# Score products of the first sixteen attention groups on all 128 rows, with each head's keys alone in a cleared buffer

## The reference

```python
x = x + layernorm(attention(layernorm(x), wq, bq, wk, bk, wv, bv, wo, bo))
x = x + layernorm(experts(layernorm(x), Ws, bs, Wg, Wu, Wd))
```

## Time and profile before

| | us |
|---|---|
| median of 3 runs | 924.04 (924.03 to 924.41) |
| the profiled execution | 925.53 |
| its span, first to last instruction | 923.4 |
| TensorE busy (share of the span) | 769.0 (83%) |
| VectorE busy | 629.2 (68%) |
| ScalarE busy | 556.9 (60%) |
| GpSimd busy | 471.1 (51%) |
| mean granted TensorE clock | 0.79 |
| mean rate of the DMA engines | 72 GB/s |

### The profile page before, as it was taken

One profiled execution on the slowest core, in us unless ns is written; L12 is line 12 of the kernel. 1 busy time (PEld: TensorE's weight loads), 2 busy tenths in 40 slices (PEclk: granted clock), 3 DMA queues, 4 the chain that ended last, 5 costly groups with the idle time before them and its releaser, 6 DMA issues. The chain is left out here.

```text
span 923.4 us, 21865 instructions
## 1 busy us (share of the span) xinstructions
PE 769.0 (83%) x6606; PEld 447.4 (48%) x6607; DVE 629.2 (68%) x2328; ACT 556.9 (60%) x1101; POOL 471.1 (51%) x540
## 2 busy tenths in 40 slices
PE   3568886789999999988998899898977999999930
PEld 1122232333333335554554455466865878778720
DVE  3855668778877787888889787755644555555546
ACT  3589887675666567665676577555543444444427
POOL 3575647475352445675366447757544223333227
PEclk9555555555555569998999899899997999999975
DMA  5343323315601011122111212212333532323248
GB/s 173 126 121 98 120 77 112 91 38 187 223 24 30 25 41 16 22 48 53 19 30 31 41 19 43 53 25 45 56 73 84 110 41 40 46 34 47 34 104 283
DMA packets 69243, 66.52 MB, mean 72 GB/s; under 512 B 5536, under 2 KB 62752, under 8 KB 69152
## 3 DMA queue, kind: packets, MB, share of 16 engines
q1 hardware_dynamic: 55872, 50.86, 17.9%
q0 software_dynamic: 13280, 14.49, 11.2%
HBM read 34.04 MB, written 31.29 MB: 71 GB/s over the span
## 5 line engine op out<-in xcount | busy, mean ns | idle before, releaser
L1035 DVE CUSTOM_DVE_ANT_0 unused<-bank,mask 128x384 f16<-128x384 f32 (+3 forms) x512 | 235.9, 485 | 83.8 <-PE bank L1408 80.7
L894 ACT ACTIVATE pT<-bank 128x512 f16<-128x512 f32 (+1 forms) x384 | 201.7, 533 | 108.9 <-PE bank L1417 105.8
L1417 PE MATMUL bank<-qT,kT 32*128 32x384 f16 (+3 forms) x512 | 176.3, 390 | 29.3 <-ACT pT L894 27.4
L1408 PE MATMUL bank<-kT,qT 32*128 32x384 f16 (+3 forms) x512 | 178.6, 398 | 8.2 <-DVE nmax L1035 7.7
L681 POOL TENSOR_SCALAR_AFFINE_SELECT pT<-pT 128x512 f16<-128x512 f16 x128 | 84.7, 706 | 129.1 <-ACT pT L894 128.4
L1837 POOL DMA_INDIRECT expert_rows<-y_sb,dest x36 | 56.0, 1555 | 118.8 <-DVE y_sb L1956 113.3
L1510 PE MATMUL bank<-tile_xT,gu_part 128*128 128x256 f16 (+1 forms) x616 | 90.0, 287 | 11.7 <-DVE stage L1219 11.6
L2031 PE MATMUL bank<-xT,gu_part 128*128 128x256 f16 (+1 forms) x792 | 94.7, 277 | 2.4 <-issue 1.4
L1417 PEld LDWEIGHTS bank<-qT,kT 32*128 32x128 f16 x512 | 39.5, 97 | 117.3 <-issue 60.6
L1448 PEld LDWEIGHTS bank<-va,pT 128*128 128x128 f16 x1280 | 49.4, 102 | 91.6 <-issue 66.7
L2031 PEld LDWEIGHTS bank<-xT,gu_part 128*128 (+1 forms) x792 | 77.9, 101 | 18.0 <-issue 3.7
(11 more groups left out here) (198 smaller groups left out, 1439.7 us busy)
## 6 DMA issues: line engine op xcount, KB each, us to landing
expert_rows<-tile_in SPq DMA_DIRECT2D x1, 8192.0 KB, 26.5
stage<-wg SPq DMA_DIRECT2D x8, 688.0 KB, 4.1
stage<-wu SPq DMA_DIRECT2D x8, 688.0 KB, 4.1
stage<-wd SPq DMA_DIRECT2D x8, 640.0 KB, 4.1
gu_part<-expert_rows SPq DMA_DIRECT2D x16, 256.0 KB, 6.5
out<-gu_part SPq DMA_DIRECT2D x16, 256.0 KB, 2.5
tile_in<-dispatch_rows SPq DMA_DIRECT2D x21, 130.0 KB
rows<-dispatch_rows SPq DMA_DIRECT2D x18, 130.0 KB
```

The lines of the kernel that those rows point to most:

```text
L894: sc.activation(pT[:, lo:hi], ST_BANK[i % 2][:, 0:hi - lo], ACT.Exp, scale=1.0 / INV_SCALE).then_inc(p_ready, 1)
L1035: last = v.tensor_tensor_reduce(out=unused[:, i % 2, at:at + n], in0=S_BANK[i % 2][:, at:at + n], in1=mask[:, T - n:T], scale=-1.0, scalar ...
L1408: last = mm(S_BANK[i % 2][:, at:at + n], qT[32 * j:32 * j + 32, g, P * qt:P * (qt + 1)], kT[32 * j:32 * j + 32, g, 0:n], start=True, stop= ...
L1417: last = mm(ST_BANK[i % 2][:, at:at + n], kT[32 * j:32 * j + 32, g, P * kt:P * (kt + 1)], qT[32 * j:32 * j + 32, g, P * kt:T], start=True, ...
```

## The change

In groups 0 to 15 both score products, and in groups 16 and 17 `scores_qk` alone, contract over all 128 partitions. The keys of head j then come from a buffer of their own, `k_alone[g][j]`, 128 partitions x 512, where all but that head's 32 partitions are zero; the queries are qT's full 128 partitions. There are 16 such buffers. They lie in memory that isn't needed yet: the last expert's weights and `tile_xT`. VectorE clears them once, with 16 memsets between the statistics and the scaling of the first norm. After each eviction of k ScalarE issues four transfers, 32 partitions x 1 KB each, from kT to the four buffers of the group (`spread_k`: three times before the first group, then at step 6 of groups 0 to 14), and TensorE waits for them before `scores_qk`. Since the last expert's weights lie there later, its three pieces (21, 22, 23) are converted in groups 16 and 17, the third loaded in batch 4, and VectorE's clearing of rows of h1 moves to the last step of group 17.

```diff
@@ -51,6 +51,7 @@
 M_MAX = B * T // TS
 WOVEN = G * B - FIRST_TILE
 GAP = 7
+HOT = 16
 EARLY_TILES = WOVEN + GAP
 LATER_TILES = TILES - EARLY_TILES
 CP = FC // 2
@@ -267,6 +268,13 @@
         ids = sb(stack, "ids", [P, QT, TOP], F32)
         spare_ids = sb(stack, "spare_ids", [P, SPARE_TILES + 1, TS // P], F32)
 
+        last_gu = [part[:, (E - 1) * KD * GU:E * KD * GU].rearrange("p (k c) -> p k c", k=KD) for part in keep["gu"]]
+        last_wd = [part[:, (E - 1) * FC * D:E * FC * D] for part in keep["wd"]]
+        alone = [part[:, k, T * m:T * (m + 1)] for part in last_gu for k in range(KD) for m in range(2)]
+        alone += [part[:, T * m:T * (m + 1)] for part in last_wd for m in range(FC * D // T)]
+        alone += [part[:, :, :].rearrange("p k t -> p (k t)") for part in tile_xT]
+        k_alone = [alone[J * g:J * (g + 1)] for g in range(G)]
+
         S_BANK, ST_BANK = (bank[0], bank[1]), (bank[2], bank[3])
         PV_BANK, Q_BANK, K_BANK, M_BANK = bank[4], bank[5], bank[6], bank[7]
         X_BANK, Y_BANK, C_BANK = K_BANK, M_BANK, Q_BANK
@@ -342,6 +350,8 @@
         dve_chain = sem("dve_chain")
         ws_chain = sem("ws_chain")
         y16_ready = sem("y16_ready")
+        alone_zero = sem("alone_zero")
+        alone_in = [sem(f"alone_in{g}") for g in range(G)]
         piece_in = [sem(f"piece_in{j}") for j in range(2)]
         hi_ready = sem("hi_ready")
         scaled_ready = sem("scaled_ready")
@@ -474,8 +484,10 @@
 
         PIECES = 3 * E
         EARLY = 6
-        PIECES_AT = {(b, g): tuple(range(EARLY + 2 * (G * b + g), min(EARLY + 2 * (G * b + g) + 2, PIECES)))
+        HELD = 3 * (E - 1)
+        PIECES_AT = {(b, g): tuple(range(EARLY + 2 * (G * b + g), min(EARLY + 2 * (G * b + g) + 2, HELD)))
                      for b in range(B) for g in range(G)}
+        PIECES_AT[HOT // G, 0], PIECES_AT[HOT // G, 1] = (HELD, HELD + 1), (HELD + 2,)
 
         def stage_of(n):
 
@@ -542,7 +554,7 @@
                     first = EARLY + 2 + 2 * G * b
 
                     def pieces(lo, hi):
-                        for n in range(first + lo, min(first + hi, PIECES)):
+                        for n in range(first + lo, min(first + hi, HELD + 2)):
                             load_piece(n)
 
                     pieces(0, 2)
@@ -550,6 +562,8 @@
                     if b < B - 2:
                         sp.wait_ge(xn_ready, b + 2)
                         load_x(x_sb, b + 2, x_in)
+                    if b == HOT // G:
+                        load_piece(HELD + 2)
                     pieces(2, 4)
                     tile_behind(G * b + 1)
                     if b:
@@ -813,8 +827,19 @@
                                              misc(key)[:, :].rearrange("p (t d) -> p t d", t=2), ACT.Copy)
                     last.then_inc(taken(key), 1)
 
+                def spread_k(of):
+
+                    wait_taken(act, ("k", of))
+                    act.wait_ge(alone_zero, 1)
+                    for j in range(J):
+                        act.dma_start(k_alone[of % G][j][32 * j:32 * j + 32, :], kT[32 * j:32 * j + 32, of % G, :]
+                                      ).then_inc(alone_in[of % G], 16)
+
                 def high_part(n):
 
+                    if n == HELD:
+                        act.wait_ge(st_mm, NF * HOT)
+                        act.wait_ge(s_mm, NF * (HOT + 2))
                     act.wait_ge(piece_in[n % 2], landed(n))
                     for dst, src in places(n, 0):
                         last = sc.activation(dst, src, ACT.Copy, scale=WSCALE)
@@ -902,6 +927,8 @@
                                 tanh(n, AT_UP[i])
                             for what, of in EVICT_AT.get(NF * grp + i, ()):
                                 evict(what, of)
+                            if i == 6 and grp + 3 < HOT + 2:
+                                spread_k(grp + 3)
                             if n >= 1 and i == 5:
                                 take_tile_y(n - 1)
                             if -1 <= n and i == AT_TILE_T:
@@ -920,6 +947,7 @@
                     evict("q", g)
                     evict("k", g)
                     evict("v", g)
+                    spread_k(g)
                 for n in range(2):
                     high_part(n)
                     scale_stage(n)
@@ -1240,7 +1268,7 @@
                                 maxima(grp + 2, (g + 2) % G, i)
                             if n >= 1 and i == 1:
                                 tile_last_low(n - 1)
-                            if (b, g, i) == (FIRST_PLAN, 0, 7):
+                            if (grp, i) == (HOT + 1, 11):
                                 dve.wait_ge(lo_ready, PIECES)
                                 v.memset(h1[P // 4:P // 2, CP - 1, TS:2 * TS], 0.0).then_inc(rows_cleared, 1)
                             if i == AT_TAKE_ATT and not (first and g == 0):
@@ -1266,7 +1294,12 @@
                                 if what == "v":
                                     bias_v(of)
 
-                for at in range(len(AT_NEXT_NORM)):
+                for at in range(3):
+                    next_norm(0, 0, at, first=True)
+                for n, rows in enumerate(alone):
+                    last = v.memset(rows, 0.0)
+                last.then_inc(alone_zero, 1)
+                for at in range(3, len(AT_NEXT_NORM)):
                     next_norm(0, 0, at, first=True)
                 dve.wait_ge(bias_ready, 2)
                 dve.wait_ge(w_in, 16 * 10)
@@ -1401,21 +1434,27 @@
                                       wv_sb[:, k, 64 * g:64 * (g + 1)], start=(k == 0), stop=(k == KD - 1))
                     last.then_inc(filled(key), 1)
 
-                def scores_qk(g, i):
-                    (j, tiles), at = S_FILLS[i], 0
+                def scores_qk(grp, i):
+                    (j, tiles), at, g = S_FILLS[i], 0, grp % G
+                    spread = grp < HOT + 2
+                    rows = slice(0, P) if spread else slice(32 * j, 32 * j + 32)
+                    keys = k_alone[g][j] if spread else kT[:, g, :]
                     for qt in tiles:
                         n = P * (qt + 1)
-                        last = mm(S_BANK[i % 2][:, at:at + n], qT[32 * j:32 * j + 32, g, P * qt:P * (qt + 1)],
-                                  kT[32 * j:32 * j + 32, g, 0:n], start=True, stop=True)
+                        last = mm(S_BANK[i % 2][:, at:at + n], qT[rows, g, P * qt:P * (qt + 1)],
+                                  keys[rows, 0:n], start=True, stop=True)
                         at += n
                     last.then_inc(s_mm, 1)
 
-                def scores_kq(g, i):
-                    (j, tiles), at = FILLS[i], 0
+                def scores_kq(grp, i):
+                    (j, tiles), at, g = FILLS[i], 0, grp % G
+                    spread = grp < HOT
+                    rows = slice(0, P) if spread else slice(32 * j, 32 * j + 32)
+                    keys = k_alone[g][j] if spread else kT[:, g, :]
                     for kt in tiles:
                         n = T - P * kt
-                        last = mm(ST_BANK[i % 2][:, at:at + n], kT[32 * j:32 * j + 32, g, P * kt:P * (kt + 1)],
-                                  qT[32 * j:32 * j + 32, g, P * kt:T], start=True, stop=True)
+                        last = mm(ST_BANK[i % 2][:, at:at + n], keys[rows, P * kt:P * (kt + 1)],
+                                  qT[rows, g, P * kt:T], start=True, stop=True)
                         at += n
                     last.then_inc(st_mm, 1)
 
@@ -1549,12 +1588,14 @@
                         if ahead:
                             wait_taken(pe, ("q", grp + 2))
                             wait_taken(pe, ("k", grp + 2))
+                            if grp + 2 < HOT + 2:
+                                pe.wait_ge(alone_in[(grp + 2) % G], 16 * J * ((grp + 2) // G + 1))
                         for i in range(NF):
                             pe.wait_ge(p_ready, NF * grp + i + 1)
-                            scores_kq(g, i)
+                            scores_kq(grp, i)
                             if ahead:
                                 pe.wait_ge(s_max, NF * (grp + 2) + i - 1)
-                                scores_qk((g + 2) % G, i)
+                                scores_qk(grp + 2, i)
                             if grp:
                                 for m in LATE_AT.get(i, ()):
                                     values(grp - 1, m)
@@ -1607,7 +1648,7 @@
                 wait_taken(pe, ("xnT", 0))
 
                 def first_scores(grp):
-                    wait_taken(pe, ("k", grp))
+                    pe.wait_ge(alone_in[grp], 16 * J)
                     for i in range(NF):
                         n = NF * grp + i
                         if n >= 2:
```

## The result

The change makes the kernel **slower**: 937.06 us (935.29 to 939.63, 4 runs) against 924.22 us (924.03 to 924.48, 4 runs), ratio 1.0138 (95% interval 1.0108 to 1.0167). On another chip the same two kernels gave 941.69 and 924.07 us, ratio 1.0218 (1.0177 to 1.0259). The profiled execution took 935.29 us, its span 933.5. The forecast was 915 us, its range ended at 934.

The account below looks back on a forecast made before the run. TensorE at half clock was taken to bound groups 9 to 15, ScalarE groups 0 to 6. Terms -9 - 2 - 6 + 3.5 + 4.3 = -9.2 us against the 924.0 us median gave 915 us, range 898 to 934.

Parts of the forecast that it names:

- pieces moved: Pieces 21 to 23 leave groups 7 and 8 (-3.9 us) and arrive in groups 16 and 17 (+3.5 us).
- four are 1.7 to 1.9 us in ScalarE's order ... exposed 1.2 us: Groups 0 to 6: four transfer issues follow step 6's exponential, which covers part; 1.2 us a group stays exposed.
- the bound of +5.8: Start: upper bound for the delay from 12 transfer issues ahead of the first group; +4.3 us was forecast.
- I take half: Groups 0 to 6: of ScalarE's 2.9 us a group waiting for scores, 1.5 us would be saved.
- The bound of +3: Groups 0 to 6: slowest case, in us, with 1.9 us of issue exposed a group; -2 us was forecast.
- Late next ... VectorE's maxima: Groups 9 to 15: with the clock up, ScalarE and VectorE's maxima come late next; TensorE sets about 8 of 12 steps.
- above 0.8: Sign that the forecast is right: granted clock above 0.8 in groups 0 to 15.
- rival B: Groups 0 to 15: the clock stays at 1.2 GHz and scores run one behind the other; 943 us, chance 0.08.
- The step from the earlier trace: TensorE's clock rises with more work on all rows, not more busy time; rise expected within group 0 or 1.
- Rival A: TensorE waits at group starts for key transfers to land, giving the gain back; 936 us, 926 with half; chance 0.18.

Follow-up runs that it names:

- number 4: Kernel before with only pieces 21 to 23 moved, the memsets and the clearing of h1 rows moved; no transfers, scores on 32 rows: 929.21 us (before 930.92).
- number 3: Changed kernel without the key transfers and the waits on them, scores on 128 rows from cleared buffers: 909.92 us (before 930.92).
- number 2: Changed kernel with all transfers and their waits kept, but all scores on 32 rows: 960.54 us (before 930.92).
- number 9: Changed kernel with each key transfer split into two of 16 partitions, so ScalarE issues eight a group: 993.25 us (before 932.19).
- number 11: Changed kernel with full rows and transfers for groups 9 to 17 alone, SyncE issuing, the 8 MB clearing in batch 3: 923.08 us (before 932.19).

## Why the prediction was wrong, by its own steps

| term, us | forecast | measured | from |
|---|---|---|---|
| pieces moved | -0.4 | +0.1 | number 4 less before |
| full rows, groups 9 to 15 | -14.7 | -10.9 | number 3 less 4 |
| full rows, groups 0 to 6 | -10.5 | -3.5 | the same |
| full rows, groups 7 and 8 | -4.0 | -3.3 | the same |
| issue, start | +4.3 | +5.7 | after less number 3 |
| issue, groups 0 to 6 | +8.4 | +13.3 | the same |
| issue, groups 7 and 8 | +1.6 | +4.5 | the same |
| issue, groups 9 to 15 | +5.6 | +9.6 | the same |

(The forecast's 2.6 - 0.5 = 2.1 and 1.5 us a group for full rows, 0.8 and 1.2 for issue, taken apart; groups 16 and 17 apart from the pieces moved by +0.4 and -0.5. The forecast's terms add up to -9.7; its -9.2 is rounded by stage.) The signs of the full rows and of the transfers were right. Two sizes were off, each by 12 to 13 us in the same direction: full rows gave 17 us in place of 29, transfers took 33 in place of 20. Those are the two steps that failed.

**Issue.** The step "four are 1.7 to 1.9 us in ScalarE's order ... exposed 1.2 us" failed twice. Its price came from the load of a weight, 0.43 to 0.48 us, and a transfer of keys takes 0.61: 2.44 for four, above the upper bound. And the cover was believed, not read. The exponential of step 6 (0.60 us) was to hide a third of the issue; number 2 less number 4 gives 13.5 us in groups 0 to 6 for 28 issues, that is 17.1 us of issue with 79% of it on the path, and the second four in number 9 aren't hidden at all (17.5 us). In a stage where ScalarE is the bound, nearly all that enters its order is paid. The upper bound for that stage had the price right, by luck: 1.9 us a group is 13.3, as measured, with four issues at 2.44 and not 1.9. It failed by the gain, below. At the start the bound of +5.8 held (+5.7).

**The gain in groups 0 to 6.** "I take half" of the 20.6 us of waiting had no row behind it. ScalarE's waits for scores fell from 20.6 us in number 4 to 17.5 in number 3, by 3.1 and not by 10 (49.2 to 164.5, and 49.3 to 161.0 us):

```profile
ACT pT L911 <- PE bank L1445: 20.6, 30, 3.6
```

```profile
ACT pT L911 <- PE bank L1445: 17.5, 27, 3.6
```

The bound of +3 kept this gain of 1.5 us a group, and so the stage lost 9.8 us. Two of the waits, the last ones of group 6, are 5.7 us in number 4 and 5.6 in number 3: there TensorE itself waits, for GpSimd's cut (2.84 us) and for VectorE's rows (2.01), which no clock of its own shortens. Of number 3's eleven other waits of over 0.5 us, nine fall in stretches where the clock is at its lower level. Its timeline shows how that comes, just after a stretch in which TensorE waited for ScalarE's scaling of a piece:

```profile
90.56 1.42 ACT L843 ACTIVATE stage<-stage 128x1376 f32<-128x1376 f32 x1
...
93.08 0.59 PE L1445 MATMUL bank<-qT,wd_part 128*128 128x512 f16 x1
...
93.46 0.63 PE L1433 MATMUL bank<-gu_part,qT 128*128 128x384 f16 x2
...
94.04 0.59 PE L1445 MATMUL bank<-qT,wd_part 128*128 128x512 f16 x1
```

A product takes 0.59 us again, so the clock has fallen, and a step takes 0.96 us. In number 3 the clock falls once a group in this stage, here in the stop that ScalarE's piece makes, and the steps that follow, in which ScalarE does wait for scores, run at the lower level with scores one behind the other. Where it stays up there was little to gain: group 1, at 0.98, took 13.7 us in place of 14.2, of which ScalarE is busy 12.5. The forecast said that the clock would fall where TensorE waits for ScalarE, and took nothing off in this stage for it.

**The gain in groups 9 to 15.** TensorE fell to 69.5 us busy, under the 80% foretold, and VectorE became the busiest (78.9 of 90.6 us). "Late next ... VectorE's maxima" was right and not priced: TensorE's waits for them in number 3 from 189.0 to 279.6 us, weights and products,

```profile
PEld bank L1433 <- DVE nmax L1052: 24.9, 42, 1.6
...
PE bank L1433 <- DVE nmax L1052: 13.1, 24, 1.4
```

where number 4 shows 2.9 and 0.6. Of the 2.6 us a group, 1.6 were to be had.

**Clock, pieces, start, landing.** The clock rose, as said (0.69 to 0.83, "above 0.8" only in the late groups); rival B is out. The step from the earlier trace rows, that the clock rises with work on all rows and not with the busy share, held here: in groups 9 to 15 number 4 keeps 0.50 at 94.5% busy, number 3 has 0.89 at 77%. With one of the two scores on 128 rows number 11 keeps 0.50 in groups 7 and 8, 99% busy. By the Trainium skill, "TensorE: Matmul & The Clock Gate", Part 1, the clock follows how busy the engine has been; these two runs differ in rows, and go the other way. The pieces came out at -4.1 and +4.7 against -3.9 and +3.5. The memsets cost nothing (49.2 us in number 4).

**Rival A** gave the time, 936 us, by luck: its landings, 15 us, were 2.7, and groups 0 to 8 lost 9.9 us more than its sum says. Its chance of 0.18 was too low because the issue's price was tied to the landing's; "slower" could come by the issue and a smaller gain alone. The range ended too low for the same two stages: groups 0 to 6 took 9.8 us more against a bound of +3, and groups 7 and 8, for which no bound was given, gave 2.9 us in place of 6. The other stages stayed within their bounds.

## What to carry to other kernels

A DMA issue is work of the engine that issues it: price it by the row of a like transfer, and where that engine is the bound, or other engines stand behind it in the order, count nearly all of it (79% in groups 0 to 6, and the whole of a second four). The same small transfers from an engine with nothing queued behind them cost 0.3 us here, unless a large transfer is in flight, on their queue above all. And a gain through the clock is only had where others wait for TensorE and nothing else stops it; look for those stops first.

## What the runs showed that was not expected

- An issue of 32 partitions x 1 KB takes 0.61 us on ScalarE and 0.59 on SyncE (medians), where a piece load takes SyncE 0.37 to 0.43. So the form of the transfer counts for more than the engine; with 16 partitions it is 0.61 too. What in the form does it wasn't tried.
- With 8 MB in flight an issue took up to 1.7 us on ScalarE's queue and up to 12.7 us behind it on SyncE's own, and a landing up to 6.7 us.
- With its scores on 32 rows TensorE kept the clock at 0.50 at 94.5% busy for 101.5 us; with them on 128 rows it had 0.89 at 77%.
- A 32-row and a 128-row score in one step lost the overlap and won no clock: +2.6 us in two groups (number 11).
